# Five places for the decay factors, and ScalarE's exponentials for them moved to the second half of each batch

## What is computed

```
x = layernorm(x + attention(x))           # causal, 16 heads of 16
x = layernorm(x + mamba(ctx, gate = x))   # a selective scan over 256 positions
x = layernorm(x + experts(x))             # 8 experts, 2 of them for each row

# the scan, for each sequence, each of 256 channels e and 16 states n:
dA[t]    = exp(delta[e, t] * A[e, n])
state[t] = dA[t] * state[t-1] + delta[e, t] * u[e, t] * B[n, t]
y[e, t]  = sum over n of C[n, t] * state[t]
```

## Time and profile before

| | |
|---|---|
| median of 3 runs | 450.21 us (450.17 to 450.51) |
| the profiled execution | 453.51 us, of which the span shown is 451.8 us |
| granted TensorE clock over the span | 0.881 of full |
| step 0 of batches 1, 2 and 3 begins (DVE L893) | 109.99, 161.33 and 212.63 us |
| last scan begins | 258.8 us |
| the experts' loop | about 293 to 429 us |

### The profile page before, as it was taken

How to read it: one execution, slowest core, us unless ns; L and a number is a source line. 1 busy time by engine, 2 the same in 40 slices (tenths; PEclk the granted TensorE clock), 3 DMA queues, 4 the chain that set the end, 5 groups by cost and what they waited for, 6 DMA issues and landing times. The chain is left out here.

```text
span 451.8 us, 5697 instructions
## 1 busy us (share of the span) xinstructions
PE 349.1 (77%) x1806; PEld 209.1 (46%) x1806; DVE 241.9 (54%) x427; ACT 216.2 (48%) x497; POOL 230.5 (51%) x221
## 2 busy tenths in 40 slices
PE   5992168768587858778576959599999999999842
PEld 3440144445244634446243524256666666666531
DVE  4025645779867796958897767412222222222224
ACT  2237776786677948777696410122222222222103
POOL 2021317669988799678988830413333333332105
PEclk9996595899678985989698679899999999999967
DMA  6004001013411161113310694001111111111062
GB/s 184 21 3 97 23 1 23 33 41 112 144 48 38 56 210 49 46 48 115 118 49 25 238 367 139 24 23 48 46 48 47 48 46 48 46 45 37 23 197 94
DMA packets 29438, 34.46 MB, mean 76 GB/s; under 512 B 4058, under 2 KB 23810, under 8 KB 29410
## 3 DMA queue, kind: packets, MB, share of 16 engines
q1 hardware_dynamic: 26114, 27.02, 19.1%
q0 software_dynamic: 2208, 6.03, 4.5%
q10 hardware_dynamic: 1088, 1.05, 0.7%
HBM read 28.92 MB, written 5.18 MB: 75 GB/s over the span
## 5 line engine op out<-in xcount | busy, mean ns | idle before, releaser
L484 POOL TENSOR_TENSOR experts<-experts,c_rows 128x1024 f32<-128x1024 f32 x31 | 73.4, 2368 | 40.6 <-DVE experts L902 40.5
L1508 PE MATMUL psS<-experts,delta 128*128 x184 | 86.5, 593 | 0.5 <-ACT delta L776 0.5
L902 DVE TENSOR_TENSOR_SCAN experts<-experts,psD 128x512 f32<-128x512 f32 x64 | 74.3, 1202 | 0.0
L547 POOL DMA_INDIRECT z_out<-delta,row_out x23 | 22.7, 988 | 88.5 <-ACT delta L790 88.5
L638 ACT ACTIVATE experts<-delta,A_sb 128x255 f32<-128x255 f32 x128 | 54.7, 516 | 2.4 <-DVE du L877 2.2
L1301 PE MATMUL psT<-ident,probs_at 128*128 128x128 f32 x192 | 37.9, 331 | 19.9 <-ACT probT L678 19.9
L1124 DVE COPY u_sb<-psD 128x512 f32<-128x512 f32 x23 | 15.9, 691 | 68.7 <-PE psD L1518 68.7
L893 DVE TENSOR_TENSOR psD<-du,psD 128x512 f32<-128x512 f32 x64 | 41.5, 687 | 13.6 <-PE psD L1260 13.3
L495 POOL TENSOR_TENSOR y_sb<-y_sb,experts 128x512 f32<-128x512 f32 x31 | 39.4, 1270 | 13.0 <-ACT y_sb L626 10.7
L1508 PEld LDWEIGHTS psS<-experts,delta 128*128 128x128 f32 x184 | 33.1, 190 | 24.3 <-issue 23.2
L487 POOL TENSOR_TENSOR experts<-experts 128x512 f32<-128x512 f32 x31 | 40.0, 1290 | 2.4
(11 more groups left out here) (228 smaller groups left out, 576.2 us busy)
## 6 DMA issues: line engine op xcount, KB each, us to landing
c_rows<-c_dram SPq DMA_DIRECT2D x32, 256.0 KB, 3.4
experts<-in_L_ffn_w_gate_dram SPq DMA_DIRECT2D x8, 512.0 KB, 5.8
experts<-in_L_ffn_w_up_dram SPq DMA_DIRECT2D x8, 512.0 KB, 6.7
experts<-in_L_ffn_w_down_dram SPq DMA_DIRECT2D x8, 512.0 KB, 8.0
x_in<-in_x_dram SPq DMA_DIRECT2D x4, 256.0 KB, 5.0
x_rows<-x_sb SPq DMA_DIRECT2D x4, 256.0 KB, 2.5
probs_at<-z_out SPq DMA_DIRECT2D x4, 256.0 KB, 5.1
c_rows<-z_out ACTq DMA_DIRECT2D x4, 256.0 KB, 6.0
```

Source lines behind the costliest of these rows:

```text
L484: pool.tensor_tensor(states[:, g % ST], states[:, g % ST], c_rows[:, g % CR].rearrange("p n (o s) -> p n o s", o=1).broadcast_to([P, 2, HA ...
L902: dve.tensor_tensor_scan(states[:, g % ST, n].rearrange("p h s -> p (h s)"), dA[:, g % DA, n].rearrange("p h s -> p (h s)"), psD[:, n, :], ...
L1508: ins = pe.matmul(psS[:, bank, :], xgT[:, s % 2, k, :], gate_up_of(bass.ds(e, 1), i)[:, k, :], start=(k == 0), stop=(k == FC - 1))
```

## The change

`dA` gets five places instead of three. The first three stay where they were; two more (`dA_more`) lie in memory of their own. The factors of steps 2 and 3 of batch 0 are made ahead of the loop as well, so that four steps' factors are ready when the loop begins. In the loop `decay` no longer stands at the beginning of each step's list: the table `DECAYS_AHEAD` says which steps' factors are made at the end of each step's attention work, after `take_o`. Steps 0 and 1 of a batch make none, step 2 makes those of step 4, step 3 those of 5, step 4 those of 6 and 7, step 5 those of the next batch's steps 0 and 1, step 6 those of its step 2, step 7 those of its step 3. In batch 3 what would belong to a fifth batch falls away.

```diff
-    DA, ST, CR, PR = 3, 5, 4, 8
+    DA, ST, CR, PR = 5, 5, 4, 8
+    SHARED = 3
+    DECAYS_AHEAD = ((), (), (4,), (5,), (6, 7), (8, 9), (10,), (11,))
...
+        dA_more = sb("dA_more", [P, DA - SHARED, 2, HALVES, S])
...
-        dA, at = carve(area, 0, DA, 2, HALVES, S)
+        dA_shared, at = carve(area, 0, SHARED, 2, HALVES, S)
...
+        def dA(i):
+            return dA_shared[:, i] if i < SHARED else dA_more[:, i - SHARED]
...
             skip(0)
             skip(1)
+            decay(2)
+            decay(3)
 
             for b in range(B):
                 f = b - 1
                 for m in range(NP):
                     g = NP * b + m
-                    if g + 2 < STEPS:
-                        if g + 2 == 2 * NP:
-                            act.wait_ge(du_rdy, TH)
-                        decay(g + 2)
                     G = GROUPS * b + m
...
                     if 1 <= m <= 4:
                         take_o(G - 1)
+                    for ahead in DECAYS_AHEAD[m]:
+                        if NP * b + ahead < STEPS:
+                            if ahead == NP:
+                                act.wait_ge(du_rdy, (b + 1) // BH + 1)
+                            decay(NP * b + ahead)
```

## The result

The changed kernel takes 472.79 us (median of 4 runs, 469.88 to 474.55), beside 450.36 us for the kernel before (4 runs, 450.17 to 454.15): **1.047 times as long, with a 95% interval of 1.039 to 1.055**. 468.8 us was predicted, with a range of 463.5 to 473.8. The medians lie 22.4 us apart and the two profiled executions (474.55 and 453.51 us) 21.0; the forecast was 18.6. The granted clock of the profiled execution is 0.860 instead of 0.881. A run over 1.5% above the fastest of its kernel counts as slow and is left out of ratios here; this concerns one run, of 473.14 us, in the experiment on the prologue. Lines of the changed kernel are numbered six higher up to about 700 and nine higher from there on: L893 (DVE's multiply) is L902, L1260 (the broadcast) is L1269, L1357 (`transpose_x2`) is L1366, L1366 (`route`) is L1375, L1338 (`project_out`) is L1347, L941 (`residual`) is L950.

A forecast was written before the change was run, and what follows sets the result against it. No engine fills the span; what counts is where decay blocks stand in ACT's way. 1.60 + 3.20 + 7.68 + 2.85 = 15.3, plus 3.3 for the clock, 18.6 us on the median 450.21: 468.8 us, range 463.5 to 473.8.

The forecast's parts named there:

- The clock bounds: PE's clock falling behind the new waits in batches 0 to 2: 3 x 1.0 to 3 x 1.6 us, 3.3 taken.
- The sign: Whole kernel: slower by more than 0.9 us, chance 0.94; within that 0.03, faster by more 0.03.
- The first half at 0: Blocks leaving steps 0 to 2: ACT's idle times behind them grow by 1.60 us each, nothing starts earlier, 0 us.
- The prologue at +1.60: Ahead of the loop: a second block delays batch 0's first exponential, and PE, DVE and ACT all follow: +1.60 us.
- Batch 0 at 3.20 + 1.1: Two blocks ahead of `take_xT` delay `project_qk` and DVE's multiply by 3.20 us; the lower clock adds 1.1.
- Batches 1 and 2 at 3.84 + 1.1 each: Blocks ahead of x2's normalisation and `take_x2T` make step 7 3.84 us late per batch; the lower clock adds 1.1.
- the third block: Batches 1 and 2: one more block ahead of `take_x2T` delays `route` and step 7, 0.64 of the 3.84 us.
- Batch 3 at +2.85: Late normalisation delays `transpose_x2` and the last step's multiply by 2.85 us; clock already down there, so nothing added.
- A clock that stays up: Rival: no clock fall behind the new waits, so 450.2 + 15.3 = 465.5 us; chance 0.22.
- One that stays low until the batch ends: Rival: low clock slows `project_qk` and `project_out`, another 2.3 us in each of three batches, 475.7 us; chance 0.09.
- That ACT has room by its 48%: Rival: ACT, busy for 48%, takes three moved blocks into its idle time; nothing changes, 450.2 us; chance 0.03.
- The gain through step 1: Rival: step 1's block does hold `take_probT`; three batches gain 1.60 us each, 447.0 us; chance 0.03.

The follow-up runs named there:

- the experiment on the prologue: The changed kernel with step 3's decay block of batch 0 behind the first exponentials instead of ahead of them: 468.69 us, 1.0362 times the kernel before.

## Why the prediction was right, step by step

The direction and the chain were right. The number came close partly by luck: terms that were 1.0 us too large in all stood beside one that was 3.3 too small, and 472.8 us lies 1.0 below the range's upper end. The clock bounds named for that end give 450.2 + 15.3 + 4.8 = 470.3 us, and "some tenths more in each batch" don't reach 473.8; no term of the sum stands for the rest.

**The sign and most of the size** came from one chain, x2 to `transpose_x2` to `project_qk` to the broadcast to DVE's multiply, and it held: the one block ahead of x2 costs 2.4% by itself, the blocks beside waits nothing that could be told (0.2%, at most 0.6), and with the two blocks moved behind x2 the multiply is back on time.

**The first half at 0** held: no gain could be told when its blocks were cut to half their time. The idle times grew as told. ACT's in batch 2, the answer to the earlier trace rows:

```profile
183.24 0.59 ACT L684 COPY probT<-psT 128x512 f32<-128x512 f32 x1 [2.26 <-PE psT L1310]
...
192.02 0.59 ACT L684 COPY probT<-psT 128x512 f32<-128x512 f32 x1 [3.09 <-PE psT L1310]
```

**The prologue at +1.60** was over-sized. The exponentials begin 1.68 us later (68.13 instead of 66.45) and `take_probT` 1.68 later too, but at the end of batch 0's attention only 0.65 us is left (`take_o` at 99.79 instead of 99.14). In the trace after, the clock is back at 1.00 in the window from 76 us, in the one before it was 0.50 until 81, and PE ran faster in between. What failed here is "all follow from these exponentials", taken at an unchanged clock.

**Batch 0 at 3.20 + 1.1** held: behind those 0.65 us, its multiply for step 6 is another 4.32 us late (106.41 instead of 101.44).

**Batches 1 and 2 at 3.84 + 1.1 each** held in the sum (4.76 and 4.59), for partly other reasons. In batch 1 `transpose_x2` stands 2.90 us later than before, counted from the batch's start, not 3.20, because the clock came back sooner in its first half; and from `transpose_x2` to the multiply it takes 3.29 us instead of 1.85, 1.44 more and not 1.1: the upper bound of the clock term. The step from step 6 to step 7 is 0.42 in batch 1 and nothing in batch 2 (0.64 predicted), and it isn't the third block that makes it. `take_x2T` starts at 162.32 and is done by 162.9, but `route` comes at 164.15 without idle time, because `project_qk` at the low clock (2.83 us) holds PE until then. So two bounds lie within 1.3 us of each other there, the block on ACT and the slow PE. With the clock held up, the block was the one that ended last (`route` waits 1.17 us for x2T at 161.66). The prediction added the 0.64 and the clock's 1.1, and its own rows say that they overlap: `take_logits` stands behind the scan of step 6, 3.45 us behind that step's multiply (155.02 less 151.57). With the multiply at 154.77 + 1.1 it can't come before 159.3, later than the 158.85 that the third block allows. So 4.3 and not 4.94 was the sum by these rows. What came out above it is, in batch 2, the clock's 1.34 us and, in batch 1, its 1.44 and the 0.42 of the slow `project_qk`.

**Batch 3 at +2.85** was the term that was mis-sized: 6.16 us. It assumed the clock to be down there already, as in the trace before. In the trace after it was full when the wait came:

```profile
266.00:268.00 2.00, 0.87 (x4) 0.37 (x4) 1.17 (x5) 2.00 (x6) 1.75 (x1) 1.00 0.00 0
268.00:270.00 2.00, 0.00 (x0) 0.00 (x0) 2.00 (x4) 2.00 (x6) 1.87 (x2) 0.80 0.00 0
...
276.00:278.00 2.00, 2.00 (x8) 1.12 (x6) 1.74 (x4) 0.45 (x1) 0.29 (x1) 0.50 1.07 384
```

```profile
270.61 1.12 PE L1366 MATMUL psT<-ident,x_sb 128*128 128x128 f32 x4 [3.30 <-ACT x_sb L697]
...
278.18 2.59 PE L1347 MATMUL psS<-wT,experts 128*128 128x256 f32 x8
```

```profile
280.81 0.69 DVE L950 TENSOR_TENSOR x<-psS,x_in 128x512 f32<-128x512 f32 x1 [1.02 <-PE psS L1347]
```

It fell and was still at 0.50 at 278 us, where before it was back at 256. Split up by the rows: 1.14 us up to the multiply of step 6 (it is there by step 3, which begins 20.94 us behind the batch's start instead of 19.70), 3.10 for the wait on x2 (`transpose_x2` 43.23 us behind the batch's start instead of 38.99, less the 1.14), 0.82 between it and the last multiply (`route` takes 1.72 us instead of 1.15), and 1.10 to `residual`, for `project_out` takes 2.59 and DVE now waits for it. The last two are matmuls at the low clock, and the 1.14 goes with a longer stretch of low clock in the first half (235 to 245 us; before, 218 to 225). Together these three make up 3.1 of the 3.3 us that the prediction lacks here. The trace of the prologue experiment, where the clock was low beforehand, has this batch 3.08 us longer than before, close to the 2.85. So this term is 3 or 6 us by where the clock happens to be, and a single number for it is a guess between the two.

**The rivals.** A clock that stays up is refuted by the 0.50 behind every new wait in batches 0 to 2. One that stays low until the batch ends is refuted for batches 0 to 2 too (1.00 from 164 us, and `project_out` at 167.23 takes 1.89), but it is nearly what happened in batch 3 (low until 279 us, `residual` at 281), which the prediction had held to be immune. That ACT has room by its 48% is refuted (nor is it the least busy by every measure: TensorE's weight loads, PEld, stand at 46%): one block of 1.6 us a batch cost 2.4% in a place where PE is short of what comes behind it, while the same blocks beside waits cost nothing that could be told. The gain through step 1 is refuted by the trace after: with the block ahead of it gone, `take_probT` comes in batch 2 11.76 us behind the batch's first multiply (183.24), and 11.74 before (173.07). The sum in the profiled pair is 20.9 us in the batches and 21.0 in all, where 18.6 was predicted: the prologue and batch 0 0.5 too much, batches 1 and 2 0.5, batch 3 3.3 too little.

## What to carry to other kernels

Ask of each instruction moved in a list what stands behind it there, who waits for that and with how much slack. The same block of 1.6 us a batch cost nothing that could be told beside a wait and 2.4% ahead of a result that the matrix engine takes up at once. Where a new wait leaves the matrix engine idle, as here for 2.15 us and more, price it twice, with the clock up and with the clock down behind it, and do so for every wait of that kind, also where the trace before shows the clock low anyway. Where a trace shows short waits of the matrix engine with a low clock behind them on the path, matmuls of no use in the wait can pay: here they were worth 1.3%. Ahead of a result that was itself late, they gave back most of what they won.

## What the runs showed of the hardware

- The clock fell behind waits shorter than I had thought: 2.09 us in the kernel before (batch 1, step 0; 0.50 in the windows from 116 to 128 us) and 2.15 us with one block ahead of x2. The rows hold no rule for it: in one kernel it fell at 164 us behind a wait of 1.17 us.
- A fall that is prevented in one place can turn up in the next: prevented at 157 us, it came at 164. The same lists gave a batch 3 of 53.43 and of 50.35 us, by the clock that the batch began its second half with.
- The kernel before took from 449.2 to 455.1 us in its runs. That this is where the clock falls in each run is only argued, from those batches, and the mean granted clock of a run doesn't order them (450.21 us at 0.887, 453.78 us at 0.893); with this spread, what is under about 0.4% could not be told here even with 19 runs of one kernel and 10 of the other.
